# Transformer layer with two expert stages on one core: setup work moved into slots between the first expert units, router logits taken from the scan state, first routed tile's weights split early

## The reference

```python
# 1. mixture of experts, gate from region means of x, top 2 of 4, plus a shared expert
gate = concat(mean(x), mean(head+proprio), mean(wrist+proprio)) @ gate_w + gate_b
gate = softmax(gate * (1 + scale) + shift)              # scale, shift from silu(cond) @ time_w + time_b
c = sum_e w[e] * mask[e] * (gelu_tanh(x @ ew1[e] + eb1[e]) @ ew2[e] + eb2[e]) + shared(x)
# 2. attention, 16 heads of 16, RMS-normed q and k, output made orthogonal to v
x = x + attention(c) @ w_proj.T
# 3. gated linear scan over the sequence, 64 states
conv = conv_b + x[t] * k1 + x[t-1] * k0
B, C = softplus(conv @ Wp[:, :64] + bp[:64]), tanh(conv @ Wp[:, 64:] + bp[64:])
state = decay * state + dt * B * (x @ Ws + bs)
h = (C * state) @ Wo + bo
# 4. routed experts, top 1 of 8
r = sigmoid(h @ Wr + br)
out = x + max(r) * (gelu(h @ W1[argmax]) @ W2[argmax])
```

## Time and profile before

| | |
|---|---|
| median of 3 executions | 872.76 us (871.27 to 2610.25) |
| profiled execution | 872.09 us |
| its span in the profile | 870.3 us |
| granted clock, mean | 0.971 |
| PE busy | 788.1 us (91%) |
| ACT busy | 525.5 us (60%) |
| DVE busy | 469.1 us (54%) |
| POOL busy | 242.8 us (28%) |

### The profile page before, as it was taken

The page is one execution under the profiler, slowest core; times in us unless marked ns, Lnnn a source line. Parts: engine busy times, 40 slices in busy tenths (PEclk is TensorE's granted clock), DMA queues, the critical chain, the costliest instruction groups (busy, mean ns, idle before and its releaser), DMA issues.

```text
span 870.3 us, 13583 instructions
## 1 busy us (share of the span) xinstructions
PE 788.1 (91%) x4472; PEld 522.9 (60%) x4472; DVE 469.1 (54%) x844; ACT 525.5 (60%) x678; POOL 242.8 (28%) x303
## 2 busy tenths in 40 slices
PE   3799999898999998879899999999889889999995
PEld 3688888776877877223222222222647578888884
DVE  5676666549866651344122111202443779999994
ACT  3222222354232224988999999998344388888883
POOL 2344444313433410600000000000000237676762
PEclk9699999999999999889999999999998999999998
DMA  7221111101132209118612440500169461111100
GB/s 194 65 49 50 48 48 48 49 1 48 30 135 104 72 0 133 13 37 182 121 37 36 73 62 11 72 0 0 49 226 378 139 221 48 50 55 51 30 11 1
DMA packets 52622, 64.87 MB, mean 75 GB/s; under 512 B 15839, under 2 KB 43877, under 8 KB 52584
## 3 DMA queue, kind: packets, MB, share of 16 engines
q1 hardware_dynamic: 47664, 58.06, 26.5%
q0 software_dynamic: 3312, 6.31, 2.4%
q10 hardware_dynamic: 1608, 0.02, 0.1%
HBM read 51.51 MB, written 15.60 MB: 77 GB/s over the span
## 4 chain that ended last, share of the span: by engine, by line
PE 59%; ACT 15%; DVE 14%; issue 9%; DVEq 1%; ACTq 1%; DMA 1%; POOLq 0%
PE psum L1360 39%; ACT pexp L793 9%; PE psum L1511 8%; PE psum L1499 4%; DVE w_lo L1292 3%; ACT w_hi L879 2%; PE psum L1562 1%; PE psum L1627 1%; DVE w_lo L1283 1%; PE psum L1679 1%; DVE yT L1120 1%; DVEq L420 1%; PE psum L1462 1%; ACT w_hi L886 1%; PE psum L1620 1%
## 5 line engine op out<-in xcount | busy, mean ns | idle before, releaser
L793 ACT ACTIVATE pexp<-psum 128x1024 f32<-128x1024 f32 x256 | 237.9, 1082 | 15.9 <-PE psum L1499 15.9
L723 ACT ACTIVATE hid<-psum,b_col 128x512 f32<-128x512 f32 x96 | 65.9, 689 | 178.8 <-PE psum L1360 111.1
L1511 PE MATMUL psum<-pexp,v_ones 128*32 128x512 f32 x1024 | 139.6, 618 | 17.9 <-ACT pexp L793 10.8
L1006 DVE TENSOR_SCALAR hh<-hid,scale_col 128x341 fp32r<-128x341 f32 x192 | 70.4, 408 | 83.3 <-ACT hid L723 63.7
L1499 PEld LDWEIGHTS psum<-q_stack,k_stack 48*128 48x128 f32 x512 | 39.8, 188 | 114.0 <-ACT pexp L793 97.2
L1499 PE MATMUL psum<-q_stack,k_stack 48*128 48x512 f32 x512 | 97.0, 454 | 9.3 <-ACT pexp L793 4.9
L920 DVE SCALAR_TENSOR_TENSOR hl<-hid,scale_col,hh 128x341 fp32r<-128x341 f32 x192 | 96.5, 544 | 3.4
L1360 PE MATMUL psum<-x_hi,w1h 128*128 128x512 f32 x192 | 77.6, 404 | 2.8 <-DVE wq_l L938 1.2
L1360 PE MATMUL psum<-hh,w2h 128*128 128x512 f32 x192 | 76.5, 398 | 3.3 <-DVE hl L920 3.2
L1360 PE MATMUL psum<-x_lo,w1h 128*128 128x512 f32 x192 | 76.1, 396 | 0.0
L1360 PE MATMUL psum<-x_hi,w1l 128*128 128x512 f32 x192 | 75.8, 395 | 0.0
(11 more groups left out here) (254 smaller groups left out, 1490.0 us busy)
## 6 DMA issues: line engine op xcount, KB each, us to landing
w_all<-in_L_ffn_W SPq DMA_DIRECT2D x16, 1024.0 KB, 12.5
raw<-in_L_cond_ew SPq DMA_DIRECT2D x32, 256.0 KB, 3.1
parts_d<-parts SPq DMA_DIRECT2D x8, 1024.0 KB, 5.0
q_stack<-parts_d SPq DMA_DIRECT2D x48, 128.0 KB, 4.8
k_stack<-parts_d SPq DMA_DIRECT2D x48, 128.0 KB, 7.7
raw<-in_L_cond_sw SPq DMA_DIRECT2D x16, 256.0 KB, 3.2
x_d<-x_tm SPq DMA_DIRECT2D x4, 1024.0 KB, 5.1
x_tm<-in_x SPq DMA_DIRECT2D x2, 1024.0 KB, 8.0
```

The costliest lines, as they stand in the source:

```text
L723: act.activation(hid[k % 4][:], bank(k % 4), ACT.Gelu_apprx_tanh, bias=b1_col[:, bass.ds(4 * q + k // 2, 1)]).then_inc(gelu_done, 1)
L793: act.activation(pexp[mt % 2][:, 2 * j:2 * j + 2, 512 * h:512 * h + 512], psum[:, 2 * r:2 * r + 2, :], ACT.Exp, scale=D ** -0.5)\
L1006: ins = dve.tensor_scalar(hh[k % 4][:, x0:x1], hid[k % 4][:, x0:x1], w[r], None, ALU.mult)
L1511: ins = pe.matmul(psum[VW * j:VW * j + VW, 6 + h, :], v_ones[i][:, mt, j, :], pexp[mt % 2][:, j, 512 * h:512 * h + 512], start=(mt == 0), ...
```

## The change

In the setup, only the four fills of the first sequence stay ahead of the experts. The other eight fills, the gate's matmuls and all of its DVE steps go into slots of the first two quads, one slot for each unit (`setup0`, `setup1`). ACT makes the region sums while it casts, in two pieces per fill, and the gate's weights are combined so that the sums can be used as they are. SP loads the shared expert's first bias, then x of sequence 0, then the first weights, then x of sequence 1. The late constants (now 19) still stand ahead of the wait for `experts_known`, and behind it the first weights of step 1 go out ahead of the remaining biases.

In the router, Wo times Wr is made ahead (two transposes, four tiny matmuls, copies on ACT), so that the logits come straight from `seq_u` in eight matmuls of 16 columns. h is made in rows at once, with bo added by a matmul of two rows, so nothing is turned back. Two of its four groups stand in PE's queue ahead of the ranks, two behind.

In the routed experts, the first tile's weights are split ahead: the high parts by ACT behind its last copies of h, the low parts of W1 by DVE behind `prob_s`, those of W2 by POOL ahead of its first gathers. The second tile's up part moves ahead of the first one's down part.

The diff, cut:

```diff
+        def setup_bank(m):
+            return bank((4, 5, 6, 7, 3, 0, 1, 2, 2, 3, 0, 1)[m])
+
         def x2_bank(w):
             return bank((2, 3, 6, 7)[w % 4])
+
+        rank_within = psum[:, 7, TT * RE:2 * TT * RE]
+        rank_total = psum[:, 7, 2 * TT * RE:3 * TT * RE]
+
+        def x3_bank(w):
+            return (0, 1, 2, 3, 4, 5, 0, 1)[w]
 
 
         parts_d = nc.dram_tensor("parts_d", [NB, 4, 2, P, L], F32).ap()
...
-            for b in range(NB):
+            def load_x(b):
                 sp.dma_start(x_tm[:, b * LT:(b + 1) * LT, :],
                              a["x"][b].rearrange("(i p) c -> p i c", p=P)).then_inc(x_in[b], 16)
-            sp.dma_start(qkv_raw[:], a["w_qkv"].rearrange("(r p) c -> p r c", p=P)).then_inc(wproj_in, 16)
-            sp.dma_start(proj_raw[:], a["w_proj"].rearrange("(r p) c -> p r c", p=P)).then_inc(wproj_in, 16)
 
 
             chosen = {}
...
+            load_x(0)
+            for k in range(2):
+                load_pair(0, 0, k)
+            load_x(1)
+            sp.dma_start(qkv_raw[:], a["w_qkv"].rearrange("(r p) c -> p r c", p=P)).then_inc(wproj_in, 16)
+            sp.dma_start(proj_raw[:], a["w_proj"].rearrange("(r p) c -> p r c", p=P)).then_inc(wproj_in, 16)
+            for k in range(2):
+                load_pair(0, 1, k)
             for dst, src in ((eb2_col[:, 0, :], a["eb2"][:, 0:P].rearrange("e p -> p e")),
                              (eb2_col[:, 1, :], a["eb2"][:, P:C].rearrange("e p -> p e")),
                              (sb2_col[:], col(a["sb2"]))):
                 sp.dma_start(dst, src, allow_slow_non_contiguous=True).then_inc(bias_in, 16)
-            for s in range(STEPS):
-                if s == 1:
...
+            sp.wait_ge(wowr_base, 1)
+            for dst, src in late_consts:
+                sp.dma_start(dst, src, allow_slow_non_contiguous=True).then_inc(late_in, 16)
+
+            def choose(s):
+                if s % 3:
+                    b, k = s // 3, s % 3 - 1
+                    chosen[s] = sp.value_load(expert_i[0:1, b, k:k + 1], min_val=0, max_val=NE - 1)
+
+            def load_b1(s):
+                src = a["eb1"][bass.ds(chosen[s], 1), :].rearrange("e f -> (e f)") if s % 3 else a["sb1"]
+                sp.dma_start(b1_col[:, s * FC:(s + 1) * FC], col(src),
+                             allow_slow_non_contiguous=True).then_inc(b1_in, 16)
+
+            sp.wait_ge(experts_known, 1)
+            choose(1)
+            for k in range(2):
+                load_pair(1, 0, k)
+            load_b1(1)
+            for s in range(2, STEPS):
+                choose(s)
+                load_b1(s)
+            for k in range(2):
+                load_pair(1, 1, k)
+            for s in range(2, STEPS):
                 for i in range(2):
...
+            x3_rows = x3_d.rearrange("(b n i p) c -> n p b i c", b=NB, n=2, p=P)
+            for n in range(2):
+                sp.wait_ge(x3_out, (n + 1) * TT // 4)
+                for b in range(NB):
+                    i0 = b * LT + LT // 2 * n
+                    sp.dma_start(x3_rows[n][:, b], x3_tm[:, i0:i0 + LT // 2, :]).then_inc(x3_stored, 16)
...
+            pool.wait_ge(late_in, 16 * LATE)
+            pool.tensor_copy(ones_r[:], ones[0:2, :])
+            pool.tensor_copy(bo_high[:], bo_row[:]).then_inc(bo_ready, 1)
+            pool.wait_ge(bo_ready, 1)
+            pool.tensor_tensor(bo_part[:], bo_high[:].bitcast(F32), pick_row[:, 1, 0:1].to_broadcast([2, C]),
+                               ALU.mult).then_inc(bo_ready, 1)
+            pool.wait_ge(bo_ready, 2)
+            pool.tensor_tensor(bo_split[:], bo_row[:], bo_part[:], ALU.subtract).then_inc(bo_ready, 1)
+            pool.wait_ge(bo_ready, 3)
+            pool.tensor_copy(bo_wide[:], wide(bo_col[:], 2, P)).then_inc(bo_spread, 1)
+
+            pool.wait_ge(x3_out, TT // 2)
+            for q in range(2):
+                pool.wait_ge(w2_hi, q + 1)
+                pool.tensor_tensor(split_quarter(w_lo, 2 + q), quarter(RE - 1, 2 + q),
+                                   split_quarter(w_hi, 2 + q).bitcast(F32), ALU.subtract).then_inc(w2_split, 1)
...
+                    for n, (x0, x1, r) in enumerate(CUTS[t]):
+                        ins = act.activation(x_hi[b][:, c, 512 * t + x0:512 * t + x1], src[:, x0:x1], ACT.Copy,
+                                             accum_out=piece_sum[:, c, b, 2 * t + n:2 * t + n + 1])
+                    ins.then_inc(hi_out, 1)
+                    return
...
+            def setup0(k):
+                if 1 <= k <= 4:
+                    hi_parts(3 + k)
+                elif k == 7:
+                    gate_softmax()
+
+            def setup1(k):
+                if 4 <= k <= 7:
+                    hi_parts(4 + k)
...
+            act.wait_ge(x2_stored, 16 * NB)
+            w1_hi_parts(0, RE - 1)
+            for q in range(2):
+                w2_hi_part(0, RE - 1, q)
             act.activation(act_warm[:], ones[0:1, 0:1], ACT.Gelu)
-            act.wait_ge(x3_stored, 16 * NB)
-            act.wait_ge(x2_stored, 16 * NB)
             act.wait_ge(slots_done, 1)
+            act.wait_ge(x3_stored, 16 * 2 * NB)
+            x_hi_part(0, 0)
+            x_hi_part(1, 1)
+            w1_hi_parts(1, place_of_expert(act, 1))
+            gelu_tile(0, 0)
...
+            by_group = gate_rows[:].rearrange("p (g k) e -> p g k e", k=CK)
+            link(dve.tensor_scalar(region_w[:, 3], by_group[:, 0], 1.0 / L, None, ALU.mult))
+            link(stt(region_w[:, 0], by_group[:, 1], 1.0 / (L - L3), region_w[:, 3], ALU.mult, ALU.add))
+            link(stt(region_w[:, 1], by_group[:, 2], 1.0 / (L - L3), region_w[:, 3], ALU.mult, ALU.add))
+            stt(region_w[:, 2], by_group[:, 2], 1.0 / (L - L3), region_w[:, 0], ALU.mult, ALU.add)\
+                .then_inc(gate_rows_in, 1)
...
+            def gate_shift():
+                dve.wait_ge(gate_summed, 1)
+                dve.tensor_tensor(gs[:, 4, 0:NE], bank(0)[0:NB, 0:NE], gs[:, 2, 0:NE], ALU.mult).then_inc(gate_read, 1)
+                dve.wait_ge(gate_read, 2)
+                link(dve.tensor_tensor(gs[:, 0, 0:NE], gs[:, 4, 0:NE], gs[:, 3, 0:NE], ALU.add))
+                link(dve.tensor_reduce(gsc[:, 0:1], gs[:, 0, 0:NE], AX, ALU.max))
+                dve.tensor_scalar(gs[:, 5, 0:NE], gs[:, 0, 0:NE], gsc[:, 0:1], None, ALU.subtract)\
...
+            def setup0(k):
+                if k < 4:
+                    lo_part(4 + k)
+                elif k == 4:
+                    gate_offset()
+                elif k == 5:
+                    gate_shift()
+                elif k == 6:
+                    gate_scores()
+                else:
+                    gate_top(0)
+
+            def setup1(k):
+                if k == 0:
+                    gate_top(1)
+                elif k == 1:
+                    gate_row()
+                elif k == 2:
+                    gate_known()
+                elif k < 6:
+                    lo_part(5 + k)
+                elif k == 6:
+                    gate_scales()
+                else:
+                    gate_biases()
+
+
+            def split_quad(q, between=None, turns_from=None, setup=None):
...
+            w1_lo_parts(0, RE - 1)
+            dve.wait_ge(x3_stored, 16 * 2 * NB)
+            x_lo_part(0, 0)
+            x_lo_part(1, 1)
+            w1_lo_parts(1, place_of_expert(dve, 1))
...
+            def modulate():
+
+                pe.wait_ge(const_in, 16 * CONSTS)
+                pe.wait_ge(gate_rows_in, 1)
+                for c in range(CK):
+                    ins = pe.matmul(bank(3)[0:NB, 0:8], sil[:, 2, c, :], time_rows[:, c, :],
+                                    start=(c == 0), stop=(c == CK - 1))
+                ins.then_inc(gate_logits, 1)
+
+            def gate():
+
+                for n in range(4):
+                    for c in range(CK):
+                        ins = pe.matmul(bank(0)[0:NB, 0:NE], piece_sum[:, c, :, n], region_w[:, (0, 1, 1, 2)[n], c, :],
+                                        start=(n == 0 and c == 0), stop=(n == 3 and c == CK - 1))
...
+            def setup0(k):
+
+                if 1 <= k <= 4:
+                    pe.wait_ge(lo_out, 4 + k)
+                elif k == 5:
+                    pe.wait_ge(gate_read, 1)
+                elif k == 6:
+                    pe.wait_ge(gate_read, 2)
+                if k < 4:
+                    if k == 0:
+                        pe.wait_ge(x_in[1], 16)
+                    fill(4 + k)
+                elif k == 4:
+                    modulate()
+                elif k == 5:
+                    gate()
+
+            def setup1(k):
+
+                if k == 3:
+                    pe.wait_ge(experts_known, 1)
+                elif 4 <= k <= 6:
+                    pe.wait_ge(lo_out, 5 + k)
+                elif k == 7:
+                    pe.wait_ge(hi_out, 12)
+                if k == 2:
+                    widen()
+                elif 3 <= k <= 6:
```

(69 more changed lines are left out.)

428 lines of the change are left out of this document (201 added, 227 removed).

## The result

The changed kernel takes 860.0 us, the median of 4 executions (858.27 to 861.06), beside 873.06 us for the kernel before on the same chip. The ratio is 0.9856, with a 95% interval of 0.9835 to 0.9877: 12.5 us or 1.4% less. One execution of the kernel before took 2610.25 us and stands outside that ratio. The forecast was 849.0 us, with a range of 841 to 859 us. The profiled execution took 859.6 us, its span is 857.8 us.

The account below looks back on a forecast made before the run. PE's matmuls were taken as the bound where work is dense, with losses at the start and router. Gains of 12.5 (start), 10.3 (middle) and 0.3 (first tile), 23.1 us, from 872.09 gave 849.0 us; 80% range 841 to 859.

Parts of the forecast that it names:

- The start: Setup up to the first expert `down`: `down` at 18.9 instead of 34.93 us, worth 12.5 us after costs.
- First gelu and its table load of 1.28 us lie under them: Setup: gelu and its table load are hidden under DVE's seven silu and gate steps of 3.0 us.
- 4.6 + 0.6 forecast: Expert slots: fills and gate work cost PE 4.6 us in full; collisions on DVE and ACT cost 0.6 us.
- the half clock: Rival, chance 0.15: in the slots PE falls to 1.2 GHz behind waits, costing 3 or 6 us; 852 to 855 us.
- The logits: Router: four matmuls behind the second half of `seq_u` take 0.92 us; DVE gets logits 13.0 us sooner.
- the ranks: Router: ranks wait behind two groups of h and reach DVE at 664.9 instead of 677.41 us, leaving 12.5 us.
- By the row I take 0.5 us off.: Router's end: POOL's W2 subtractions slow DVE by only 0.5 us, as in an earlier hh pair, leaving 10.3 us.
- The rows of h are no later ... 675.5 us.: Ahead of the first gather: last rows at 670.4 us, a store lands in 5.1 us, so they don't delay it.
- The first tile: Routed experts: weights ready and the second `up` moved ahead gain 0.3 us, with 0 and 1.5 as ends.
- The second tile's casts still wait for the first one's `up`: First tile of the routed experts: this limits the gain there to 0.3 us.
- POOL holds DVE: Rival, chance 0.14: two POOL subtractions block DVE at the end of its router chain, 4.8 us for 0.5; 853 us.
- It doesn't do what it says: Rival, chance 0.05: ACT, SP or late folded weights undo the logits' gain; only the start is left, 860 us.

Follow-up runs that it names:

- `table_early`: The changed kernel with a one-element gelu behind silu's exponential, so that gelu's table loads there; 859.09 us (0.9837).
- `tile_old_order`: The changed kernel with its first FFN tile in the order of the kernel before; 859.41 us (0.9851).
- `w2_behind_x`: `stores_ahead` with DVE's two W2 subtractions placed behind the first tile's `x_lo`; 855.86 us (0.9807).
- `stores_ahead`: `w2_on_dve` with two experts' weight loads moved from ahead of h's stores to behind the first gathers; 855.08 us (0.9801).
- `w2_on_dve`: The changed kernel with POOL's two W2 subtractions for the first tile moved to DVE; 857.25 us (0.9829).
- `warm_mid`: The changed kernel with 12 in place of 7 warming matmuls ahead of the lanes, 5 behind as before; 857.83 us (0.9837).

## Why the prediction was wrong

The mechanisms were nearly all there, and the gain was half of the sum. By its steps:

- **The start, 12.5 us forecast, 10.5 measured.** x and the weights were right within 0.1 us, and the four fills were through at 13.4 us for 14.0. "First gelu and its table load of 1.28 us lie under them" failed: the load stands behind gelu's wait. The first pair of hh took 1.60 us beside POOL, not 0.62. The first `down` came at 19.98 us, 1.1 us late. `table_early` shows that the load itself was worth 0.2 us at the end of the stage; the executions whose first `up` ran at 0.23 us a matmul (18.25 to 18.56 us) ended it 0.6 to 1.5 us earlier. The other 0.9 us is the slots: from the first `down` to the last `y_lo` pieces it is 134.0 us, against 129.6 before less the clock's 1.7, so 6.1 us for 4.6 + 0.6 forecast. In the slots the half clock did not return: PEclk is 1.00 from 20 to 62 us, and twelve matmuls took 2.75 us.
- **The logits, 13.0 us forecast, 12.2 measured (22.9 - 10.7), the ranks 12.5 forecast, 11.3 measured.** The four logit matmuls behind the second half took 1.77 us, not 0.92; their twins of the first half, at full clock, took 1.06. The clock was down behind PE's wait for `seq_u` of 1.63 us, and the two groups of h ahead of the ranks ran at 0.50 too. In `tile_old_order` and `w2_behind_x` the same wait, 1.62 us, left the clock up: from the end of `seq_u` to ACT's sigmoid it is 1.49 us, here 2.19. So the wait alone doesn't explain it.
- **The first failing step: "By the row I take 0.5 us off."** The hold cost 2 x 2.15 = 4.3 us on `tile_hot` alone. The row was misread. Its pair of hh ran from 43.08 us, and the last of POOL's subtractions beside it ended 0.68 us later, so the row's 0.47 us came from a short overlap, not from a mild hold. In the changed kernel a pair of hh beside two whole subtractions, 1.5 us of overlap, took 1.60 us for 0.62. I had the rule, gave it 0.14, and put its place at `lane_hot`. POOL's pieces started where the forecast had them: its 673.4 us, less the scan's 10.7 us, is 662.7, and they started at 662.43. DVE's chain was the later one, by the 1.2 us at the ranks, so the hold fell on two products of `tile_hot` and not on `lane_hot`.
- **The second failing step: "The rows of h are no later ... 675.5 us."** Less the scan's 10.7 us this is 664.8 us; the last store landed at 672.5. Its 5.1 us from issue to landing is the row of the kernel before; behind 12 MB of weights the four stores took 8.1 to 12.1 us, and 2.9 to 4.1 in `stores_ahead`, with 4 MB less ahead of them. The hold hid this by 0.7 us. With the hold gone (`w2_on_dve`) the gather stood 23.7 us behind the start of the second `seq_u`, for 21.1 forecast (679.7 - 658.65).
- **A step that was missing: work behind a long wait ran at the half clock.** I let the clock fall in the slots alone, as a rival, and nowhere in the router. PE, kept from the lanes for 4.59 us, dropped to the half clock; lanes and warming matmuls took 3.39 and 6.45 us, for 2.13 and 4.54 in `warm_mid`. At the first turn the gain was 14.9 us, 4.4 beyond the start where 10.3 was forecast.
- **The first tile, +0.3 us forecast, -2.2 measured** (14.9 to 12.7 us). "The second tile's casts still wait for the first one's `up`" was right, but the new order puts them ahead of gelu, 0.6 us, and PE fell to the half clock behind them, 1.6 us.
- **The rival that came true** is "POOL holds DVE", 853 us, with its price right (4.8 for 4.3 us); the half clock was a rival for the slots alone, and came at the logits, the lanes and the second `up`. "It doesn't do what it says", 860 us, has the number by luck: the logits' gain was real, and neither ACT nor the folded weights held anything. But its other half, that SP holds the rows of h, was 0.7 us from being the limit and became it as soon as the hold was gone.

The parts add up: 2.0 (start) + 5.9 (logits to first turn) + 2.5 (first tile) = 10.4 us of the missing 10.6. The rest of the middle was forecast well. From the start of the second `seq_u` to the first turn it is 30.6 us in the changed kernel, where the forecast had 34.85 - 10.3 = 24.6, and 24.1 in `stores_ahead`, without the hold and the late stores. What `stores_ahead` still lacks to 849 us lies in the start, in the first tile and in the late gather.

Two things stay open: which waits cost PE its clock, in the first `up`, at the logits and in the first tile, and why executions of the stretch up to `seq_u` get a different clock.
